# A one-layer language-model tower on one core: block 0's layer norms split between two engines, the first recurring pass written out

## Chip, core and metric

The kernel runs on one core of a Trainium2 chip. The metric is the device time of one launch in microseconds (us), as the median of several runs. The core's engines are TensorE (PE in the profile), VectorE (DVE), ScalarE (ACT), GpSimd (POOL) and SyncE (SP), which here only issues DMAs. Each engine works through its own list of instructions in order, and waits on semaphores for the others.

## What is computed

The input is an (8, 1024) array of token numbers: L = 8 positions, N = 1024 sequences, width 256. The reference, cut to what matters:

```
h = take(table, x)                                   # (8, 1024, 256)
h = h + attention(layernorm(h))                      # 16 heads of 16, softmax over the 8 positions
h = h + ffn(layernorm(h))

attention:  qkv = x @ Wqkv.T + b;  softmax(q k / 4) v @ Wo.T + bo
ffn:        scores = sigmoid(x @ Wg.T); 2 of 4 groups, then 4 of 16 experts by scores + bias
            weights = 2.5 * scores / sum(scores of the 4)
            sum over experts of weight * W2[e] relu(W1[e] x)^2  +  Ws2 relu(Ws1 x)^2
layernorm:  (x - mean) / sqrt(var + 1e-5)
```

Everything is float32. Each operand of most matmuls is split into a high part (rounded to fp32r) and a low part (the rest), and three products are summed.

## The kernel before

**Tiling.** The 1024 sequences are cut into B = 16 blocks of 64, so that a block has 512 tokens, held either as rows (128 partitions x 4 rows j x 256) or transposed (128 partitions x 2 halves kh x 512). For each block: `gather` (GpSimd, L395) fetches the rows into `xin`; `norm_stats` (VectorE, L755) takes the statistics; `rstd_of` (GpSimd, L405) makes scale and shift from them in eight small operations, a power and a product; `normalise` (ScalarE, L538) writes the four normalised rows; `transpose_rows` (TensorE, L1177) transposes them into PSUM; `transposed_hi` (ScalarE, L549) and `transposed_lo` (VectorE, L763) split them; `qkv` (L1191) and `qkv_out` (L558) give q, k and v. `product` (VectorE, L288) multiplies q and k into a ring of four buffers, `score` (L1206) sums over a head, `scores_max`, `exponent`, `scores_sum`, `probs_high`, `probs_low` are the softmax. `spread_probs` (L1222) spreads probabilities over lanes, `weighted_values` (L769) multiplies them with v, `sum_of` (L304, on GpSimd or VectorE) sums over positions, `attention_hi`/`_lo` split the result, `out_projection` (L1240) and `residual` (L897) give h1, with the statistics of the second norm right behind. The second norm takes the same path (w = 1) to xT2. Then `logits`, `logits_back`, 22 steps of `route` on VectorE, `weights_transpose` and `weights_out`, a store and reloads of the expert weights by SP (L355, L349), and for each of 18 hidden tiles (2 shared, 16 experts) `up` (L1145), `weigh` on VectorE (L731), `square` on ScalarE (L524), `hidden_lo` on VectorE (L742) and `down` (L1160).

**Weights.** They come in 14 pieces. SP issues their loads (L324 to L345), from piece 4 on after the first block's rows have landed. `weight_hi(k)` (ScalarE, L519) rounds a piece and `weight_lo(k)` (VectorE, L726) makes the rest. The pieces are staged in buffers that are used for other things later: the ring holds pieces 4 to 8, so the first product waits until nine pieces are done (RING_FREE, L281), and SP stores block 0's expert weights only after thirteen (L379).

**Order of the work.** Each engine has a list written out by hand, which has two parts: a start-up list for block 0, block 1 and the beginning of the expert work of block 0, and then `for b in range(B + 1): period(b)`. One `period(b)` interleaves the expert work of block b with the second half of the attention of block b + 1 and the first half of that of block b + 2. The start-up lists stand at L489 (GpSimd), L673 (ScalarE), L1056 (VectorE) and L1386 (TensorE). `warm(4)` (L1277) in TensorE's list is four matmuls on a weight piece whose result is never read; there are 17 such calls.

**GpSimd's start.** It issues the gathers of blocks 0 and 1 (eight in all, L495 and L497), then does `rstd_of(0, 0)`, `constants_small` (masks), `constants_spread` (a memset and four selects on a 128 x 1024 buffer, L457) and `bias_in(0)` (L427), which adds the output bias to `xin` and waits for the broadcasts of the biases.

Of the kernel before, what the change touches and what calls it, by code (L numbers as in the profile page):

```python
# [5 lines left out]
def lm_tower_layer(nc: bass.Bass, ids, table, wqkv_t, bqkv, wo_t, bo, wg_t, bias_corr,  # L6
# [8 lines left out]
    f32 = mybir.dt.float32  # L15
# [44 lines left out]
    with ctx:  # L60
# [99 lines left out]
        xn_ready = [sem("xn1_ready"), sem("xn2_ready")]  # L160
        xT_mm = [sem("xT1_mm"), sem("xT2_mm")]
# [224 lines left out]
        def _(pool):  # L386
# [18 lines left out]
            def rstd_of(w, blk):  # L405
                st, m = stats[w], mv[w]
                tt, ts = nc.gpsimd.tensor_tensor, nc.gpsimd.tensor_scalar
                pool.wait_ge(ln_stats[w], nth(blk, 1, 1))
# [3 lines left out]
                pool.wait_ge(ln_step[w], nth(blk, 5, 1))  # L412
# [3 lines left out]
                pool.wait_ge(ln_step[w], nth(blk, 5, 2))  # L416
                tt(m[:, 1, :], m[:, 1, :], m[:, 1, :], ALU.mult).then_inc(ln_step[w], 1)
                pool.wait_ge(ln_step[w], nth(blk, 5, 3))
                tt(m[:, 2, :], m[:, 2, :], m[:, 1, :], ALU.add).then_inc(ln_step[w], 1)
                pool.wait_ge(ln_step[w], nth(blk, 5, 4))  # L420
                if blk >= 1:
                    pool.wait_ge(xn_ready[w], nth(blk, 1, 0))
                tt(rstd[w][:, :], m[:, 2, :], half_neg[:, :], ALU.pow).then_inc(ln_step[w], 1)
                pool.wait_ge(ln_step[w], nth(blk, 5, 5))
                tt(nmr[w][:, :], m[:, 3, :], rstd[w][:, :], ALU.mult).then_inc(ln_rstd[w], 1)

            def bias_in(blk):  # L427
# [3 lines left out]
                pool.wait_ge(xn_ready[0], nth(blk, 1, 1))  # L431
                par = blk % 2
# [76 lines left out]
            bias_in(1)  # L509
# [3 lines left out]
            for b in range(B + 1):  # L513
                period(b)
# [3 lines left out]
        def _(act):  # L518
# [19 lines left out]
            def normalise(w, blk):  # L538
# [5 lines left out]
                for j in range(TT):  # L544
# [4 lines left out]
            def transposed_hi(w, blk):  # L549
                act.wait_ge(xT_mm[w], nth(blk, 1, 1))  # L550
# [5 lines left out]
                nc.scalar.copy(dst[:, :, :], src[:, :, :]).then_inc(xT_hi[w], 1)  # L556
# [133 lines left out]
            weight_hi(9)  # L690
            qkv_out(0, 5)
            spread_in()
# [5 lines left out]
            weight_hi(11)  # L698
            transposed_hi(0, 1)
            attention_hi(0, 1)  # L700
            qkv_out(1, 0)
            qkv_out(1, 1)
            qkv_out(1, 2)
            qkv_out(1, 3)
            weight_hi(12)
            qkv_out(1, 4)
            normalise(1, 0)
            weight_hi(13)
            transposed_hi(1, 0)
            logits_out(0)  # L710
            router(0)
# [771 lines left out]
```

## Time and profile before

| | us |
|---|---|
| median of 3 runs | 1248.94 |
| lowest, highest | 1248.72, 1251.21 |
| profiled execution, its time | 1247.4 |
| profiled execution, span of the core's instructions | 1245.7 |
| busy in that span: TensorE, VectorE, ScalarE, GpSimd | 1198.8, 1021.5, 597.0, 503.8 |

The profile is of one execution. All times in its rows are counted from the first instruction. A timeline row merges like instructions that follow one another on an engine (x4) and gives start, duration, engine, line, operation, what is written from what, and in brackets how long the engine had been idle before and what released it. `<-` in a name reads "from". The granted clock (PEclk) is TensorE's, as a share of full speed.

### The profile page before, as it was taken

What the parts mean: (1) busy time and instruction counts of PE and PEld (TensorE: products, weight loads), DVE (VectorE), ACT (ScalarE), POOL (GpSimd) and SP (SyncE); (2) the same over time, 40 slices, a digit from 0 to 9 for tenths busy, and PEclk for the clock granted to TensorE, in tenths of its full rate; (3) what the DMA queues carried; (4) which work ended last, traced back from release to release, by engine and by line L of the source; (5) the groups of instructions that cost most, each with busy time, mean ns of one, the idle gap of its engine ahead of it and who ended that gap; (6) DMA issues with size and microseconds to landing.
All of it is one profiled execution on the core that took longest, in us unless ns stands there. A gap on an engine that the chain in (4) does not pass through costs nothing.

```text
span 1245.7 us, 19787 instructions
## 1 busy us (share of the span) xinstructions
PE 1198.8 (96%) x7428; PEld 1013.5 (81%) x7428; DVE 1021.5 (82%) x1732; ACT 597.0 (48%) x1056; POOL 503.8 (40%) x717
## 2 busy tenths in 40 slices
PE   3689999999999999999999999999999999999998
PEld 3357888797888878788887888879788887878897
DVE  4989798897979889787888978788897878888643
ACT  4334645454464545446454544544455454444443
POOL 7355435163542516354251635425263451516000
PEclk9898999999999999999999999999999999999999
DMA  6002222032222213222121322213132221312232
GB/s 225 1 18 69 70 68 89 31 105 67 86 69 69 75 45 104 68 87 68 57 82 51 103 68 86 69 30 108 52 102 69 72 82 34 104 35 91 64 108 63
DMA packets 34127, 91.64 MB, mean 74 GB/s; under 512 B 4720, under 2 KB 13296, under 8 KB 34032
## 3 DMA queue, kind: packets, MB, share of 16 engines
q1 hardware_dynamic: 30960, 81.99, 20.2%
q0 software_dynamic: 3072, 8.39, 2.2%
q8 instruction: 58, 0.95, 0.3%
q14 instruction: 37, 0.30, 0.1%
HBM read 81.46 MB, written 8.91 MB: 73 GB/s over the span
## 4 chain that ended last, share of the span: by engine, by line
PE 93%; DVE 4%; POOL 1%; issue 1%; ACT 1%; DMA 0%; DVEq 0%; POOLq 0%; ACTq 0%; SPq 0%
PE psY L1170 33%; PE psH L1155 32%; PE psB L1201 10%; PE psB L1217 4%; PE psA L1248 4%; PE psB L1236 2%; PE psA L1236 2%; PE psA L1260 1%; DVE ring L288 1%; PE psB L1187 1%; PE psA L1187 1%; PE psY L1281 1%; POOL xin L401 1%; PE psA L1274 1%; PE psA L1267 0%
## 5 line engine op out<-in xcount | busy, mean ns | idle before, releaser
L1170 PE MATMUL psY<-w_hi,hid_hi 128*128 128x256 f32 x1152 | 326.1, 283 | 0.0
L1170 PE MATMUL psY<-w_hi,hid_lo 128*128 128x256 f32 x1152 | 323.8, 281 | 0.0
L1170 PE MATMUL psY<-w_lo,hid_hi 128*128 128x256 f32 x1152 | 323.3, 281 | 0.0
L534 ACT ACTIVATE p_sb<-r_sb 128x512 f32<-128x512 f32 x288 | 181.2, 629 | 255.1 <-DVE r_sb L739 212.5
L536 ACT ACTIVATE hid_hi<-r_sb 128x512 fp32r<-128x512 f32 x288 | 180.0, 625 | 215.4 <-PE psY L1170 212.8
L739 DVE SCALAR_TENSOR_TENSOR r_sb<-psH,cwB 128x512 f32<-128x512 f32 x256 | 173.7, 684 | 83.3 <-PE psH L1155 79.1
L1170 PEld LDWEIGHTS psY<-w_hi,hid_hi 128*128 128x128 f32 x1152 | 217.0, 188 | 20.9 <-DVE hid_lo L745 11.7
L1155 PE MATMUL psH<-xT_hi,w_hi 128*128 128x512 f32 x576 | 230.8, 401 | 1.2 <-ACT r_sb L529 1.2
L1155 PE MATMUL psH<-xT_hi,w_lo 128*128 128x512 f32 x576 | 228.5, 397 | 0.0
L1155 PE MATMUL psH<-xT_lo,w_hi 128*128 128x512 f32 x576 | 227.8, 395 | 0.0
L1170 PEld LDWEIGHTS psY<-w_lo,hid_hi 128*128 128x128 f32 x1152 | 216.9, 188 | 9.3
L745 DVE TENSOR_TENSOR hid_lo<-p_sb,hid_hi 128x512 fp32r<-128x512 f32 x288 | 199.0, 700 | 22.9 <-ACT hid_hi L536 20.9
L1170 PEld LDWEIGHTS psY<-w_hi,hid_lo 128*128 128x128 f32 x1152 | 216.8, 188 | 0.0
L310 POOL TENSOR_TENSOR ring<-ring 128x512 f32<-128x512 f32 x94 | 144.1, 1533 | 93.0 <-DVE ring L777 92.1
L438 POOL TENSOR_TENSOR w_rec<-w_sum,half_neg 128x4 f32<-128x4 f32 x16 | 24.2, 1514 | 380.3 <-DVE w_sum L846 380.3
L288 DVE TENSOR_TENSOR ring<-q_sb,k_sb 128x1024 f32<-128x1024 f32 x128 | 153.4, 1224 | 4.1 <-ACT k_sb L567 3.9
L1155 PEld LDWEIGHTS psH<-xT_hi,w_hi 128*128 128x128 f32 x576 | 108.8, 189 | 33.5 <-DVE r_sb L739 10.9
L1155 PEld LDWEIGHTS psH<-xT_hi,w_lo 128*128 128x128 f32 x576 | 108.8, 189 | 25.6
L1155 PEld LDWEIGHTS psH<-xT_lo,w_hi 128*128 128x128 f32 x576 | 109.0, 189 | 19.1
L777 DVE TENSOR_TENSOR ring<-psA,v_sb 128x1024 f32<-128x1024 f32 x64 | 78.1, 1220 | 10.0 <-PE psA L1236 9.9
L777 DVE TENSOR_TENSOR ring<-psB,v_sb 128x1024 f32<-128x1024 f32 x64 | 77.9, 1218 | 7.2 <-PE psB L1236 7.2
L401 POOL DMA_INDIRECT xin<-table,idx x64 | 73.3, 1145 | 19.1 <-issue 17.2
(138 smaller groups left out, 1854.3 us busy)
## 6 DMA issues: line engine op xcount, KB each, us to landing
cwB<-cw_dram SPq DMA_DIRECT2D x128, 512.0 KB, 3.7
out<-h SPq DMA_DIRECT2D x32, 256.0 KB, 3.2
xin<-table,idx POOLq DMA_INDIRECT x64
ring<-w_t SPq DMA_DIRECT2D x4, 256.0 KB, 6.3
h<-w_t SPq DMA_DIRECT2D x2, 512.0 KB, 7.6
ring<-w_t SPq DMA_DIRECT2D x1, 512.0 KB, 6.6
p_sb<-w_t SPq DMA_DIRECT2D x2, 256.0 KB, 7.0
cwB<-w_t SPq DMA_DIRECT2D x1, 512.0 KB, 7.8
```

Source lines behind the costliest of these rows:

```text
L288: ns.tensor_tensor(ring[:, t % 4, :, :].rearrange("p l (m n) -> p l m n", m=L), qv.unsqueeze(2).to_broadcast([P, 2, L, NN]), kv.unsqueeze( ...
L310: ns.tensor_tensor(a[:, :, 0:4, :], a[:, :, 0:4, :], a[:, :, 4:8, :], ALU.add).then_inc(sum_step[who], 1)
L401: nc.gpsimd.indirect_dma_start(xin[b % 2][:, j, :], None, table, bass.IndirectOffsetOnAxis(idx[:, b * TT + j:b * TT + j + 1], 0)).then_inc ...
L534: nc.scalar.activation(p_sb[:, n % 2, :], r_sb[:, n % 2, :], ACT.Square)
L536: nc.scalar.activation(hid[0][:, n % R, :], r_sb[:, n % 2, :], ACT.Square).then_inc(hid_hi, 1)
L739: nc.vector.scalar_tensor_tensor(r_sb[:, n % 2, :], psH[:, n % 2, :], 0.0, cwB[:, (r // QN) % 2, r % QN, :], ALU.max, ALU.mult).then_inc(w ...
L745: nc.vector.tensor_tensor(hid[1][:, n % R, :], p_sb[:, n % 2, :], hid[0][:, n % R, :].bitcast(f32), ALU.subtract).then_inc(hid_lo, 1)
L777: nc.vector.tensor_tensor(ring[:, t % 4, :, :], ps[:, :, :], v_sb[:, ih, :].unsqueeze(1).to_broadcast([P, 2, T]), ALU.mult).then_inc(av_re ...
L1155: last = nc.tensor.matmul(psH[:, n % 2, :], W1[a][:, kh, e, :], x[c][:, kh, :], start=(kh == 0 and (a, c) == PASSES[0]), stop=(kh == KH - ...
L1170: last = nc.tensor.matmul(psY[:, j // 2, (j % 2) * D:(j % 2 + 1) * D], hid[a][:, e % R, j * P:(j + 1) * P], W2[b][:, e, :], start=(e == 0 ...
L1201: last = nc.tensor.matmul(psB[:, n % 2, :], WQKV[a][:, kh, 2 * c + ih, :], xT1[b][:, kh, :], start=(kh == 0 and (a, b) == PASSES[0]), stop ...
L1217: last = nc.tensor.matmul(psB[row:row + 32, 0, :], head_sum[:, lp, :], ring[:, (KH * lp + ih) % 4, li, :], start=(lp == 0), stop=(lp == LP ...
```

## The change

**Normalisation of block 0, both layer norms.** `norm_stats` calls the new `first_norm` for block 0. The mean and variance come from `bn_aggr` on VectorE, GpSimd only raises to the power -1/2, VectorE makes the shift, and then VectorE normalises rows 2 and 3 while ScalarE normalises rows 0 and 1. TensorE signals after the first four of eight transposes, ScalarE makes the high part in two halves and VectorE the low part in two halves. Later blocks go the old way.

**Order.** On GpSimd `constants_small` and `rstd_of(0, 0)` come ahead of the gathers of block 1, and `bias_in(0)` ahead of `constants_spread`. On the other engines several steps of the start-up lists change places, and the first recurring pass, `period(0)`, becomes part of the list, with an order of its own; the loop starts at 1. TensorE's list has 17 calls of `warm(4)` before and after, at other places: one instead of two after the first transposes, three ahead of the transposes of the second norm of block 0, none behind the first `spread_probs(1, ...)`.

The diff, with the lists cut to the places that the prediction speaks of:

```
             def rstd_of(w, blk):
+                if blk == 0:
+                    pool.wait_ge(first_step[w], 2)
+                    tt(rstd[w][:, :], m[:, 2, :], half_neg[:, :], ALU.pow).then_inc(first_root[w], 1)
+                    return
...
 # GpSimd's list
             gather_first(0)
+            constants_small()
+            rstd_of(0, 0)
             gather_first(1)
-            rstd_of(0, 0)
-            constants_small()
+            bias_in(0)
             constants_spread()
-            bias_in(0)
             sum_of(0, 0)
...
             gather(2)
-            bias_in(1)
             root_of_sum(0)
             sum_of(1, 0)
             sum_of(1, 1)
-            for b in range(B + 1):
+            sum_of(1, 2)
+            bias_in(1)
+            rstd_of(0, 2)
...
+            for b in range(1, B + 1):
                 period(b)
...
             def normalise(w, blk):
-                for j in range(TT):
+                for j in range(TT if blk > 0 else TT // 2):
...
             def transposed_hi(w, blk):
+                if blk == 0:
+                    to, ps = (xT1[0], psB) if w == 0 else (xT2[0][0], psA)
+                    act.wait_ge(half_mm[w], 1)
+                    nc.scalar.copy(to[:, 0, :], ps[:, 0, :]).then_inc(half_hi[w], 1)
                 act.wait_ge(xT_mm[w], nth(blk, 1, 1))
...
-                nc.scalar.copy(dst[:, :, :], src[:, :, :]).then_inc(xT_hi[w], 1)
+                if blk == 0:
+                    nc.scalar.copy(dst[:, 1, :], src[:, 1, :]).then_inc(xT_hi[w], 1)
+                else:
+                    nc.scalar.copy(dst[:, :, :], src[:, :, :]).then_inc(xT_hi[w], 1)
...
 # ScalarE's list
+            weight_hi(4)
             normalise(0, 0)
-            weight_hi(4)
             weight_hi(5)
+            transposed_hi(0, 0)
             weight_hi(6)
-            transposed_hi(0, 0)
             weight_hi(7)
             qkv_out(0, 0)
             weight_hi(8)
...
+            weight_hi(11)
             probs_high(0)
             normalise(0, 1)
+            transposed_hi(0, 1)
             attention_hi(0, 0)
...
             def norm_stats(w, blk):
+                if blk == 0:
+                    first_norm(w)
+
+            def first_norm(w):
+                src, dst = (xin[0], k_sb) if w == 0 else (h1[0], o_sb)
+                m = mv[w]
...
+                dve.wait_ge(ln_stats[w], 1)
+                for j in range(TT):
+                    last = nc.vector.bn_aggr(pairs[:, j, :], stats[w][:, j, :])
+                last.then_inc(first_step[w], 1)
+                dve.wait_ge(first_step[w], 1)
+                nc.vector.tensor_scalar(m[:, 2, :], var, EPS, None, ALU.add).then_inc(first_step[w], 1)
+                dve.wait_ge(first_root[w], 1)
+                nc.vector.scalar_tensor_tensor(nmr[w][:, :], mean, -1.0, rstd[w][:, :], ALU.mult, ALU.mult
+                                               ).then_inc(ln_rstd[w], 1)
+                dve.wait_ge(ln_rstd[w], 1)
...
+                for j in range(TT // 2, TT):
+                    last = nc.vector.tensor_scalar(d[:, j, :], src[:, j, :], rstd[w][:, j:j + 1], nmr[w][:, j:j + 1],
+                                                   ALU.mult, ALU.add)
+                last.then_inc(first_rows[w], 1)
...
             def transposed_lo(w, blk):
+                if blk == 0:
+                    dve.wait_ge(half_hi[w], 1)
+                    nc.vector.tensor_tensor(dst[1][:, 0, :], src[:, 0, :], dst[0][:, 0, :].bitcast(f32), ALU.subtract)
+                    dve.wait_ge(xT_hi[w], 1)
+                    nc.vector.tensor_tensor(dst[1][:, 1, :], src[:, 1, :], dst[0][:, 1, :].bitcast(f32),
+                                            ALU.subtract).then_inc(xT_lo[w], 1)
...
 # VectorE's list
+            weight_lo(10)
+            probs_low(0)
             norm_stats(0, 1)
-            probs_low(0)
...
+            transposed_lo(0, 1)
             weighted_values(0, 7)
-            transposed_lo(0, 1)
...
             product(1, 2)
+            transposed_lo(1, 0)
             product(1, 3)
...
-            hidden_lo(0, 0)
+            weight_lo(12)
             weighted_values(1, 0)
+            hidden_lo(0, 1)
             weighted_values(1, 1)
-            for b in range(B + 1):
+            weighted_values(1, 2)
+            weighted_values(1, 3)
+            norm_stats(0, 2)
+            weigh(0, 2)
...
+            attention_lo(1, 1)
+            product(2, 0)
+            hidden_lo(0, 7)
+            weight_lo(13)
+            residual(1)
+            weigh(0, 8)
...
             def transpose_rows(w, blk):
+                if blk == 0:
+                    pe.wait_ge(first_rows[w], 1)
...
+                    if blk == 0 and kh == 0:
+                        last.then_inc(half_mm[w], 1)
...
 # TensorE's list
             transpose_rows(0, 0)
             warm(4)
-            warm(4)
             qkv(0, 0)
...
             qkv(0, 4)
+            qkv(0, 5)
             score(0, 0)
...
+            qkv(1, 2)
             out_projection(0)
...
+            down(0, 0)
             spread_probs(1, 0)
             weights_transpose(0)
             spread_probs(1, 1)
-            warm(4)
-            for b in range(B + 1):
+            spread_probs(1, 2)
+            spread_probs(1, 3)
+            down(0, 1)
+            spread_probs(1, 4)
+            spread_probs(1, 5)
+            up(0, 3)
+            up(0, 4)
...
+            qkv(2, 4)
+            up(0, 10)
...
+            for b in range(1, B + 1):
                 period(b)
```

## Rows read from the trace of the kernel before

**Rows 1.** The chain that ended last, by engine.
```profile
PE 93%; DVE 4%; POOL 1%; issue 1%; ACT 1%; DMA 0%; DVEq 0%; POOLq 0%; ACTq 0%; SPq 0%
```

**Rows 2.** Windows by stage; the first line names the columns.
```profile
core 0: us, PE busy (x) PEld busy (x) DVE busy (x) ACT busy (x) POOL busy (x), PEclk, DMA share, GB/s
...
67.17:104.44 37.27, 31.60 (x147) 21.79 (x147) 31.16 (x59) 15.46 (x27) 14.78 (x16) 0.86 0.05 15
...
104.90:175.80 70.90, 70.23 (x436) 58.92 (x435) 60.89 (x107) 34.20 (x62) 31.34 (x44) 1.00 0.21 68
175.80:249.00 73.20, 73.20 (x462) 62.22 (x461) 62.35 (x107) 36.42 (x66) 31.08 (x44) 1.00 0.23 73
```

**Rows 3.** Waits of TensorE from 105 us on, longest of three (total, times, longest).
```profile
PE psA L1187 <- ACT o_sb L545: 1.3, 1, 1.3
```

**Rows 4.** Timeline of the head: start us, duration us, engine, line, operation, idle before.
```profile
10.55 1.41 DVE L760 BATCH_NORM_STATS2 stats<-xin 128x6 f32<-128x256 f32 x4 [1.92 <-DMA xin<-table,idx]
...
12.81 0.95 POOL L401 DMA_INDIRECT xin<-table,idx  x1 [0.30 <-issue]
...
15.74 1.05 POOL L423 TENSOR_TENSOR rstd<-mv,half_neg 128x4 f32<-128x4 f32 x1
...
19.33 1.94 PE L1187 MATMUL psB<-ident,k_sb 128*128 128x128 f32 x8 [19.33 <-POOL not_first L453]
20.93 3.34 PE L1281 MATMUL psY<-wqkv_hi 128*128 128x512 f32 x8
```

**Rows 5.** Timeline, VectorE beside GpSimd; a line's durations (ns min/median/max); VectorE's products.
```profile
21.20 1.57 DVE L729 TENSOR_TENSOR w_lo<-ring,w_hi 128x1024 fp32r<-128x1024 f32 x1 [0.18 <-ACT w_hi L522]
22.70 1.21 DVE L766 TENSOR_TENSOR xT_lo<-psB,xT_hi 128x1024 fp32r<-128x1024 f32 x1
...
27.44 2.35 DVE L729 TENSOR_TENSOR w_lo<-ring,w_hi 128x1024 fp32r<-128x1024 f32 x1 [1.94 <-ACT w_hi L522]
29.90 9.17 DVE L288 TENSOR_TENSOR ring<-q_sb,k_sb 128x1024 f32<-128x1024 f32 x8
...
26.30 2.41 POOL L433 TENSOR_TENSOR xin<-xin,bo_sb 128x1024 f32<-128x1024 f32 x1
...
L463 POOL TENSOR_SCALAR_AFFINE_SELECT r_sb<-r_sb x4: 845/1488/1602, 20.4 to 24.6; 128x512 f32<-128x512 f32 x4
```

**Rows 6.** Issues on SP's queue; page part 6: issues, size, median us to landing.
```profile
13.76 0.65 SPq L343 DMA_DIRECT2D bias_corr_sb<-bias_corr  x1
14.45 1.32 SPq L330 DMA_DIRECT2D ring<-w_t  x2
...
ring<-w_t SPq DMA_DIRECT2D x4, 256.0 KB, 6.3
...
bias_corr_sb<-bias_corr SPq DMA_DIRECT2D x1, 8.0 KB, 6.7
```

**Rows 7.** Timeline of VectorE and ScalarE, block 0's second half and block 1's products.
```profile
65.91 1.21 DVE L766 TENSOR_TENSOR xT_lo<-psB,xT_hi 128x1024 fp32r<-128x1024 f32 x1
...
76.07 1.41 DVE L760 BATCH_NORM_STATS2 stats<-h 128x6 f32<-128x256 f32 x4
...
86.80 1.22 DVE L766 TENSOR_TENSOR xT_lo<-psA,xT_hi 128x1024 fp32r<-128x1024 f32 x1
...
91.46 1.13 DVE L796 TENSOR_TENSOR lgt<-lg 128x64 f32<-128x64 f32 x1 [1.17 <-ACT lg L601]
...
98.07 0.41 DVE L824 MAX8 top<-cho 128x8 f32<-128x16 f32 x4
...
81.36 2.08 ACT L545 ACTIVATE o_sb<-h,nmr,rstd 128x256 f32<-128x256 f32 x4
```

**Rows 8.** Timeline from the end of block 1's probabilities.
```profile
103.00 1.39 DVE L884 TENSOR_TENSOR probs<-s_sb,probs 64x512 fp32r<-64x512 f32 x2
...
112.14 0.69 DVE L739 SCALAR_TENSOR_TENSOR r_sb<-psH,cwB 128x512 f32<-128x512 f32 x1 [0.85 <-DMA cwB<-cw_dram]
...
113.59 0.40 PE L1155 MATMUL psH<-xT_hi,w_hi 128*128 128x512 f32 x1
```

More of the change, by code:

```diff
@@ L1103, in _ @@
             product(1, 5)
-            weight_lo(12)
-            transposed_lo(1, 0)
+            route(0, 0)
             product(1, 6)
-            weight_lo(13)
-            route(0, 0)
+            route(0, 1)
             product(1, 7)
-            route(0, 1)
             route(0, 2)
@@ L1121, in _ @@
             route(0, 11)
+            scores_max(1)
             route(0, 12)
             route(0, 13)
+            route(0, 14)
             scores_sum(1)
-            route(0, 14)
             route(0, 15)
+            hidden_lo(0, 0)
             route(0, 16)
@@ L1133, in _ @@
             route(0, 21)
-            hidden_lo(0, 0)
+            weight_lo(12)
             weighted_values(1, 0)
+            hidden_lo(0, 1)
             weighted_values(1, 1)
-            for b in range(B + 1):
+            weighted_values(1, 2)
+            weighted_values(1, 3)
+            norm_stats(0, 2)
+            weigh(0, 2)
+            weigh(0, 3)
+            weighted_values(1, 4)
+            weigh(0, 4)
+            weigh(0, 5)
+            weighted_values(1, 5)
+            hidden_lo(0, 2)
@@ new lines, in _ @@
+            sum_of(1, 3)
+            hidden_lo(0, 3)
+            hidden_lo(0, 4)
+            attention_lo(1, 0)
+            weigh(0, 6)
+            weighted_values(1, 6)
+            hidden_lo(0, 5)
+            weigh(0, 7)
+            weighted_values(1, 7)
+            transposed_lo(0, 2)
+            sum_of(1, 7)
+            hidden_lo(0, 6)
+            attention_lo(1, 1)
[4 more added lines that the diff above has]
+            weigh(0, 8)
@@ new lines, in _ @@
+            weigh(0, 9)
+            hidden_lo(0, 8)
+            product(2, 1)
+            product(2, 2)
+            product(2, 3)
+            product(2, 4)
+            weigh(0, 10)
+            hidden_lo(0, 9)
+            transposed_lo(1, 1)
+            weigh(0, 11)
+            weigh(0, 12)
+            hidden_lo(0, 10)
+            product(2, 5)
+            route(1, 0)
+            hidden_lo(0, 11)
+            route(1, 1)
+            product(2, 6)
+            route(1, 2)
+            weigh(0, 13)
@@ new lines, in _ @@
+            product(2, 7)
+            route(1, 3)
+            route(1, 4)
+            hidden_lo(0, 12)
+            route(1, 5)
+            route(1, 6)
+            scores_max(2)
+            hidden_lo(0, 13)
+            route(1, 7)
+            weigh(0, 14)
+            route(1, 8)
+            route(1, 9)
+            route(1, 10)
+            weigh(0, 15)
+            route(1, 11)
+            hidden_lo(0, 14)
+            route(1, 12)
+            weigh(0, 16)
+            route(1, 13)
@@ new lines, in _ @@
+            route(1, 14)
+            scores_sum(2)
+            hidden_lo(0, 15)
+            route(1, 15)
+            route(1, 16)
+            route(1, 17)
+            route(1, 18)
+            weigh(0, 17)
+            hidden_lo(0, 16)
+            route(1, 19)
+            probs_low(2)
+            route(1, 20)
+            route(1, 21)
+            hidden_lo(0, 17)
+            weighted_values(2, 0)
+            hidden_lo(1, 0)
+            weighted_values(2, 1)
+            for b in range(1, B + 1):
@@ L1393, in _ @@
             qkv(0, 4)
+            qkv(0, 5)
             score(0, 0)
-            qkv(0, 5)
+            warm(4)
             score(0, 1)
@@ L1409, in _ @@
             warm(4)
+            warm(4)
             spread_probs(0, 6)
```

169 lines of the change are left out of this document (135 added, 34 removed).

## The prediction

> **What bounds the kernel now.** I read the chain that ended last first, since it says which engine sets the end: TensorE has 93% of it [rows 1]. Next the windows, by stage. From the second pass on TensorE is busy 73.20 us of 73.20, and in the first pass (104.90 to 175.80) 70.23 of 70.90, while VectorE has ten free microseconds or more; in the stretch before, 67.17 to 104.44, it is busy 31.60 of 37.27 us at a granted clock of 0.86, with VectorE at 31.16 [rows 2]. The waits of TensorE after 105 us then have three entries, the longest 1.3 us [rows 3]. So the kernel has two parts: up to about 104 us VectorE and chains of short steps bound it, with TensorE often idle or on `warm` matmuls that compute nothing; behind that TensorE's fixed work runs without a gap. A microsecond taken out before 104 us is a microsecond off the end, unless TensorE gets a gap later. I forecast by following the first 113 us. The profiled execution has a span of 1245.7 us and a time of 1247.4 us, 1.5 us under the median of 1248.94; the sum is made on the first and shifted by 1.5.
>
> **Head: first normalisation (0 to 39 us).** Today the statistics end at 11.96 us (10.55 + 1.41), but GpSimd still issues the second block's gathers until 13.76, then needs eight small operations up to 15.74 (about 0.25 each), the power of 1.05 and a product, to 17.1; behind ScalarE's four rows (2.08 in the second norm [rows 7]) the transposes start at 19.33 [rows 4]. The change puts those gathers behind the power. On VectorE four `bn_aggr` come in, which no row shows: nearest are the four MAX8 of 0.41 in all [rows 7], the other end the four statistics themselves, 1.41; I take 0.41, because the inputs are 6 elements wide. With one `tensor_scalar` (0.2), the power (1.05), one product (0.2) and five hand-overs of some 0.07, scale and shift stand at 14.2 instead of 17.1. ScalarE does two rows (half of 2.08) and VectorE two beside it (at most 0.35 each by the statistics' rate): transposes at 15.4, 3.9 earlier. The halves let the high part follow the first four transposes, so xT_lo is there at 18.3; four warm matmuls (today eight take 3.34 [rows 4], so 1.7) end at 18.7: the first qkv moves from 24.3 to 18.7.
>
> That is not what the head gains. The products also need the ring's weight piece 8. Its loads are issued from 14.45 on and take 6.3 us in the middle [rows 6], so it lands near 21.6; cast (1.04) and qkv_out(0,1) (0.7) follow, at 23.4. On VectorE pieces 6, 7 and 8 queue. `bias_in(0)` now starts when its broadcasts land, issued 13.76, 0.65 long, 6.7 to landing: 20.5 [rows 6]. Today piece 8 takes 2.35 beside it [rows 5]; tomorrow piece 7 meets it. `constants_spread` moves behind it, to about 23 to 30. Product 0 so starts between 24.9 (ScalarE and the load) and 26.0 (with the blocks beside `bias_in`); I take 25.4 against 29.90.
>
> The eight products take 9.17 [rows 5] in free air; three of the four selects now lie beside them. A piece beside a select took 1.57, while an instruction of the same size with a PSUM operand took 1.21 [rows 5]: 0.35 extra. A select took 0.845 at least and 1.6 at most. I take 0.6 a select, 1.9 with the memset's end: last product 36.5 instead of 39.07, **-2.6 us**. Bounds: -5.0 with no collision, -0.5 if each of four products takes the 2.35 of the piece beside `bias_in`.
>
> The Trainium skill ("SBUF — State Buffer", section "Who interferes with whom") says that a VectorE instruction with two SBUF inputs and a GpSimd instruction that reads SBUF exclude each other for a whole instruction, and speaks against this move. By it three selects cost 2.5 us instead of 1.9; the trace agrees: `bias_in` ended at 28.71 and piece 8, begun at 27.44, ended 1.1 later [rows 5].
>
> **Middle (39 to 75 us).** Moving `norm_stats(0,1)` (1.4) behind `probs_low(0)` fills the 1.3 us in which VectorE waits for the first spread, and weight_lo(10) takes its old place beside probs_high: nothing gained or lost here, 1.1 saved later. transposed_lo(0,1), at 65.91 today [rows 7], passes one weighted_values (1.2), so qkv(1,0) starts 1.1 earlier. Out-projection now stands behind three qkv but these start earlier; the residual stays behind weight_lo(11): **-1.0**, bounds 0 and -1.2.
>
> **Second normalisation (76 to 104 us).** Today statistics end 77.48, GpSimd's chain gives the shift at 81.3, ScalarE starts at 81.36 and VectorE's low part at 86.80, behind product 5 and weight_lo(12) [rows 7]. After: chain of 2.1 instead of 3.8, rows 1.04 instead of 2.08, transposes 3.7 earlier (the twelve warm matmuls ahead end 0.3 before); VectorE, held 2.1 us for the power, does products 1 and 2 and then the two low halves of about 0.65: logits 5.2 earlier (82.9 without the head's gain). From there to the end of probs_low(1) VectorE needs 16.4 us today (88.02 to 104.39 [rows 7, 8]). After: three products more (+3.45), weight_lo(13) gone (-1.15), the 1.17 us wait for the logits filled, the first route step 0.9 shorter without `bias_in(1)` beside it [rows 7], hidden_lo(0,0) in front (+0.6): 17.6. So probs_low(1) ends at 100.5, 3.9 earlier with the middle, of which **-2.9** here. Bounds: -1.5 (if `bn_aggr` costs 1.41 and TensorE's steps run at half speed) and -4.
>
> **Recurring pass 0 (104 to 176 us).** Its clock starts at T = end of probs_low(1). Today up(0,4) starts at T + 9.2, right after weigh(0,2), which waits for the expert weights' table until T + 7.75 [rows 8]; TensorE has done five spreads, up 3, down 0 and 1, and four warm matmuls. After: weight_lo(12) (1.2) stands before the first weighted value, four of these and the statistics before weigh(0,2), which ends at T + 8.8; TensorE has done the same and one spread more (0.47): **-0.8**. Bounds +3 and -2. weight_lo(13) goes into VectorE's free time. The table's DMAs keep their place, after cwT, since weight_lo(12) ends before cwT is ready. The semaphores themselves I cost at nothing.
>
> Sum: -2.6 - 1.0 - 2.9 - 0.8 = -7.3; 1247.4 - 7.3 = 1240.1, and 1241.6 as a median.
>
> **Rivals.**
> A. The forecast, 1238 to 1244: 0.68.
> B. The head gives nothing: weight_hi(4) now stands before the normalisation on ScalarE, and its load is issued at 10.54; a landing after 14.2, or the collisions at their upper bound, eats it. Speaking for it: loads issued two microseconds later take 6.3 [rows 6]; against: the DMA engines carry far less at that moment, and the loads at piece 8 hide 2 us of it anyway. -7.3 + 2.6 = -4.7: 1244.2. The skill's rule above, taken in full, ends here too. 0.11.
> C. TensorE at the lower of its two levels. It ran matmuls at 0.42 instead of 0.23 us in the warm group at 20.93 [rows 4], and had 0.86 granted in 67 to 104 [rows 2]. It idles some 2 us in the first 9 of the new pass; if the low level reaches eight microseconds into the pass, 4 are lost: 1245.6. 0.09.
> D. No change: the gain is handed back by gaps in the pass that was written out, 1248.9. Against it: ten free microseconds of VectorE [rows 2]. 0.06.
> E. Slower. Place: up(0,10), which needs weigh(0,8), now behind residual(1), product(2,0) and weight_lo(13) on VectorE. By my count weigh(0,8) ends at T + 35 and TensorE gets there at T + 37.3, 2.3 of slack. Each microsecond beyond costs one; it decides for slower from 2.3 + 7.3 + 2.5 = 12 us of delay, i.e. if all VectorE work of that stretch took a third longer. With 14 us: 1251.0 or more. 0.06.
>
> **How the numbers follow.** A measurement can tell 0.2% (2.5 us) from no change. A, B and C are faster, 0.88; D same, 0.06; E slower, 0.06. The range of 1238 to 1246.5 holds A to C but for their tails, and leaves out D and E.
>
> **What would show it.** Right: POOL's power at 12.8 instead of 15.74; transposes near 15.4; first product near 25.4 and the last one's end near 36.5; products of 1.5 to 2.1 us beside the selects; first logits near 80; probs_low(1) ending near 98; up(0,4) some 9 us later; in the pass TensorE idle for at most 2 us. Wrong: a long wait of ScalarE before its first row (B), a granted clock under 1.00 after the start of the pass (C), waits of TensorE on r_sb or hid_lo in the 70 us after it (D, E).

## The result, and the profile after

The changed kernel takes 1240.35 us, the median of 4 runs (1238.81 to 1241.86), against 1249.30 for the kernel before (1248.72 to 1251.21): a ratio of 0.9927, with a 95% interval of 0.9913 to 0.9941. The forecast was 1241.6 us in a range of 1238.0 to 1246.5.

The profiled execution of the changed kernel has a time of 1241.86 us and a span of 1240.1; that of before 1247.4 and 1245.7. The two profiles so differ by 5.5 us and the medians by 9.0: the profile of before is one of its faster executions, that of after the slowest of its four. The second profile of the changed kernel, below, shows what part of this the trace can explain. All steps below are read from the profiles.

| mark in the trace, us | before | after | after, a second profile |
|---|---|---|---|
| transposes of the first norm start | 19.33 | 15.22 | 15.18 |
| first product starts | 29.90 | 24.57 | 24.54 |
| first maximum of the softmax (`scores_max(0)`) | 40.37 | 38.16 | 37.26 |
| residual(0) | 74.82 | 71.30 | 70.42 |
| probs_low(1) ends (T) | 104.39 | 96.93 | 96.06 |
| `weights_transpose(1)`, the end of the first recurring pass | 175.9 | 170.4 | 169.0 |
| end of the span | 1245.7 | 1240.1 | 1238.7 |

From the second pass on each pass takes 73.1 to 73.2 us in all three (the last one 62.3 to 62.4), so whatever stands at 170 us stands at the end. By stage, against before: head -2.2, middle -1.3, second normalisation -3.9, first recurring pass **+1.9** us, sum -5.5.

The page of after: the chain that ended last, by engine, and the busy line. They answer to [rows 1]; VectorE's share of the chain went from 4 to 6%, TensorE's busy time is the same to a tenth.

```profile
PE 1198.8 (97%) x7428; PEld 1012.1 (82%) x7428; DVE 1028.3 (83%) x1750; ACT 593.5 (48%) x1054; POOL 505.2 (41%) x699
...
PE 91%; DVE 6%; issue 1%; POOL 1%; ACT 1%; DMA 0%; POOLq 0%; DVEq 0%; SPq 0%
```

VectorE's timeline in the head of after (start, duration, operation, idle before and its releaser):

```profile
12.02 0.38 DVE L838 BATCH_NORM_AGGREGATE mv<-stats 128x2 f32<-128x6 f32 x4
...
14.03 0.73 DVE L848 TENSOR_SCALAR k_sb<-xin,rstd,nmr 128x256 f32<-128x256 f32 x2
...
18.76 5.70 DVE L794 TENSOR_TENSOR w_lo<-ring,w_hi 128x1024 fp32r<-128x1024 f32 x3 [0.25 <-ACT w_hi L545]
24.57 11.42 DVE L293 TENSOR_TENSOR ring<-q_sb,k_sb 128x1024 f32<-128x1024 f32 x8
...
38.16 0.69 DVE L959 TENSOR_REDUCE s_max<-psB 128x64 f32<-128x512 f32 x1 [1.03 <-PE psB L1400]
```

GpSimd's in the same stretch:

```profile
12.75 1.04 POOL L415 TENSOR_TENSOR rstd<-mv,half_neg 128x4 f32<-128x4 f32 x1 [1.75 <-DVE mv L841]
...
18.88 3.37 POOL L445 TENSOR_TENSOR xin<-xin,bo_sb 128x1024 f32<-128x1024 f32 x1
...
23.29 7.12 POOL L475 TENSOR_SCALAR_AFFINE_SELECT r_sb<-r_sb 128x512 f32<-128x512 f32 x4
```

The four aggregates take 0.38 us (taken: 0.41) and the power starts at 12.75 (forecast 12.8). The three pieces take 5.70 instead of 3 x 1.2 because `bias_in(0)` meets them, and is itself stretched to 3.37 from 2.41 [rows 5] (2.92 in the second profile, where it started 0.4 later). The eight products take 11.42 instead of 9.17 [rows 5], 2.25 more, beside the four selects. The last one ends at 35.99; the forecast was 36.5.

TensorE in after, the last three scores of the head; then windows of after and of before around them (busy us and count of TensorE, its weight loads, VectorE, ScalarE, GpSimd, then the granted clock, the DMA share and GB/s):

```profile
31.60 1.07 PE L1400 MATMUL psB<-ring,head_sum 128*32 128x512 f32 x8 [1.34 <-DVE ring L293]
33.87 1.93 PE L1400 MATMUL psB<-ring,head_sum 128*32 128x512 f32 x8 [1.20 <-DVE ring L293]
36.14 1.93 PE L1400 MATMUL psB<-ring,head_sum 128*32 128x512 f32 x8 [0.34 <-DVE ring L293]
```

```profile
30.00:39.00 9.00, 5.19 (x26) 0.64 (x24) 7.94 (x8) 2.57 (x3) 0.41 (x1) 0.69 0.01 2
```

```profile
33.00:42.00 9.00, 6.29 (x38) 2.26 (x34) 8.59 (x9) 2.75 (x4) 0.00 (x0) 1.00 0.01 2
```

The eight matmuls of each of the last two scores take 1.93 us instead of 1.07: TensorE had been waiting for stretched products, and its clock fell to the lower of its two levels, 1.2 GHz (0.69 on the mean of these nine microseconds, 1.00 before). The last score thus ends 0.9 later. In the second profile of the same kernel the scores took 1.06 us behind the same waits (1.20 and 1.21), and the softmax began 0.9 earlier; the marks of the table ahead of it differ by at most 0.04.

The second norm in after, VectorE. It answers to [rows 7]:

```profile
71.30 1.23 DVE L1000 TENSOR_TENSOR h<-psA,xin 128x1024 f32<-128x1024 f32 x1 [1.07 <-issue]
72.56 1.41 DVE L825 BATCH_NORM_STATS2 stats<-h 128x6 f32<-128x256 f32 x4
...
78.83 0.68 DVE L856 TENSOR_TENSOR xT_lo<-psA,xT_hi 128x512 fp32r<-128x512 f32 x1
...
95.54 1.39 DVE L980 TENSOR_TENSOR probs<-s_sb,probs 64x512 fp32r<-64x512 f32 x2
```

From the residual to the low part it is 7.5 us instead of 12.0, and to the end of probs_low(1) 25.6 instead of 29.6.

Windows of after: the 32.5 us ahead of the pass, the pass, the next one, and two stretches of the pass's opening. They answer to [rows 2].

```profile
65.00:97.50 32.50, 29.57 (x161) 20.58 (x159) 29.19 (x68) 14.40 (x26) 12.67 (x6) 1.00 0.06 17
97.50:170.40 72.90, 70.52 (x419) 58.15 (x419) 63.58 (x107) 34.49 (x62) 33.89 (x45) 0.98 0.20 66
170.40:243.60 73.20, 73.20 (x462) 62.27 (x461) 63.70 (x108) 36.36 (x67) 32.09 (x44) 1.00 0.23 73
...
103.00:104.00 1.00, 1.00 (x7) 1.00 (x6) 1.00 (x2) 0.00 (x0) 1.00 (x1) 0.50 0.87 315
104.00:105.00 1.00, 1.00 (x6) 1.00 (x6) 1.00 (x4) 0.00 (x0) 0.84 (x3) 0.50 0.77 315
```

TensorE's waits in the pass (longest of those from 96 us on):

```profile
PE psA L1419 <- DVE ring L873: 1.0, 1, 1.0
...
PE psA L1419 <- ACT cwT L603: 0.7, 1, 0.7
PE psB L1419 <- DVE probs L980: 0.6, 1, 0.6
```

The pass that was written out is 72.9 us instead of 70.9: TensorE idles 2.4 of them (0.7 before [rows 2]), at its start, between spreads, and for three microseconds around 103 us it has 0.50 granted.

### The profile page after: what moved, and what is told of

It is laid out like the page before. It is cut to its first block, busy times and chain, and to the rows that moved or that the text cites. A ratio compares the mean times of both kernels' runs of the same rounds, so it can differ in the third digit from the quotient of the medians.

```text
span 1240.1 us, 19788 instructions
## 1 busy us (share of the span) xinstructions
PE 1198.8 (97%) x7428; PEld 1012.1 (82%) x7428; DVE 1028.3 (83%) x1750; ACT 593.5 (48%) x1054; POOL 505.2 (41%) x699
## 4 chain that ended last, share of the span: by engine, by line
PE 91%; DVE 6%; issue 1%; POOL 1%; ACT 1%; DMA 0%; POOLq 0%; DVEq 0%; SPq 0%
PE psY L1349 33%; PE psH L1334 32%; PE psB L1384 10%; PE psB L1400 4%; PE psA L1431 4%; PE psA L1419 2%; PE psB L1419 2%; DVE ring L293 1%; PE psA L1443 1%; PE psB L1368 1%; PE psA L1368 1%; DVE ring L873 1%; DVE w_lo L794 1%; PE psA L1457 1%; PE psA L1450 0%
## 5 line engine op out<-in xcount | busy, mean ns | idle before, releaser
L810 DVE TENSOR_TENSOR hid_lo<-p_sb,hid_hi 128x512 fp32r<-128x512 f32 x288 | 201.7, 709 | 23.9 <-ACT hid_hi L559 22.1
L1334 PEld LDWEIGHTS psH<-xT_hi,w_lo 128*128 128x128 f32 x576 | 108.3, 188 | 25.4
L406 POOL DMA_INDIRECT xin<-table,idx x64 | 77.5, 1212 | 18.9 <-issue 16.8
```

What stands on the lines that cost most here:

```text
L406: nc.gpsimd.indirect_dma_start(xin[b % 2][:, j, :], None, table, bass.IndirectOffsetOnAxis(idx[:, b * TT + j:b * TT + j + 1], 0)).then_inc ...
L810: nc.vector.tensor_tensor(hid[1][:, n % R, :], p_sb[:, n % 2, :], hid[0][:, n % R, :].bitcast(f32), ALU.subtract).then_inc(hid_lo, 1)
L1334: last = nc.tensor.matmul(psH[:, n % 2, :], W1[a][:, kh, e, :], x[c][:, kh, :], start=(kh == 0 and (a, c) == PASSES[0]), stop=(kh == KH - ...
```

## The experiments

The kernel before ran again beside each group; its medians were 1248.82, 1248.18, 1247.69 and 1248.79 us. "T" is the end of probs_low(1) in the experiment's own profile (before 104.39, after 96.93). Line numbers are each kernel's own.

### Group 1: which part earns the gain

**The new normalisation alone**: the functions of after, the four lists of before.

```
-            constants_small()
-            rstd_of(0, 0)
             gather_first(1)
-            bias_in(0)
+            rstd_of(0, 0)
+            constants_small()
             constants_spread()
+            bias_in(0)
...
-            for b in range(1, B + 1):
+            for b in range(B + 1):
                 period(b)
```

> The new code for block 0 (bn_aggr, shared rows, halves) with all four lists of the kernel before. Theory 1 (the gain is the earlier end of probs_low(1), and each part gives what lies on the path): GpSimd's gathers of block 1 still stand ahead of the power, so the transposes start near 16.2 instead of 19.33 and the first product near 27 instead of 29.9; in the second norm VectorE's low part stands behind product 5 and weight_lo(12) as before, so the faster chain gives nothing there. Total about -3 us, ratio 0.9975. Theory 2 (the normalisation is the whole gain): -7 us or more, ratio 0.994 or below. Rival: nothing, because VectorE is held for the power: ratio 1.000.

1246.92 us, ratio 0.9991 (0.9978 to 1.0005). The first norm's transposes start at 16.24 (3.1 earlier, still behind the second block's gathers), but the softmax only 1.1 earlier, at 39.24, and T is 100.95. In the second norm the low part starts at 84.21, 2.6 earlier, no more than the residual's own 2.7: it stays behind product 5 and weight_lo(12), so the norm gains nothing up to there.

**The order alone**: all four lists of after, the functions of before.

> The old normalisation code with all four new lists (so the written-out pass too). Theory 1: the chain of the first norm starts at 12 instead of 13.8 and one warm group is gone, the selects still meet the products; low part of the second norm before product 3; about -4 to -5 us, ratio 0.996 to 0.997, and together with the norm-only kernel about the whole change. Theory 2 (normalisation is the whole gain): ratio 0.999 to 1.001.

1248.92 us, ratio 1.0003 (0.9991 to 1.0014). VectorE's timeline says why:

```profile
76.67 2.34 DVE L288 TENSOR_TENSOR ring<-q_sb,k_sb 128x1024 f32<-128x1024 f32 x2
87.16 1.22 DVE L812 TENSOR_TENSOR xT_lo<-psA,xT_hi 128x1024 fp32r<-128x1024 f32 x1 [8.15 <-ACT xT_hi L567]
88.30 3.48 DVE L288 TENSOR_TENSOR ring<-q_sb,k_sb 128x1024 f32<-128x1024 f32 x3
```

The new order puts transposed_lo(1, 0) behind two products, which fits a normalisation that is ready by then. The old one isn't: VectorE stands 8.15 us with five products queued behind. By the medians either part alone gives 1.9 us, with an interval that holds 1.000, or nothing; the two together give 9. (Between its profile and that of before, the normalisation alone gives 3.4 us, at T and at the end of the span.) Order and code are one change.

**The loop's first pass**: after, with `period(0)` of the loop instead of the pass written out (weight_hi(13), weight_lo(13) and bias_in(1) ahead of it, down(0, 0) inside it).

```
             sum_of(1, 1)
-            sum_of(1, 2)
             bias_in(1)
...
-            for b in range(1, B + 1):
+            for b in range(B + 1):
                 period(b)
...
             weighted_values(1, 1)
-            weighted_values(1, 2)
-            weighted_values(1, 3)
-            norm_stats(0, 2)
-            weigh(0, 2)
...
             weight_lo(13)
...
```

> The changed kernel, but with the first recurring pass taken from the loop as before (start-up list cut before down(0,0), weight pieces 12 and 13 and bias_in(1) ahead of the loop). The forecast's step (the written-out pass gives 0.8 us) wants it about 1 us slower than the changed kernel, ratio to before 0.9935. The reading of the trace of after (the pass took 72.9 us between two weights_transpose although 2.35 us of matmuls were taken out of it, so its opening loses some 2.8 us) wants it equal or up to 2 us faster, ratio 0.991 to 0.993, with TensorE idle under 1 us in the first 10 us behind the end of probs_low(1).

1242.87 us, ratio 0.9958 (0.9944 to 0.9972); T is 97.05, and the pass takes 74.4 us against 72.9. TensorE's two longest waits from 96 us on:

```profile
PE psB L1290 <- DVE probs L934: 2.8, 1, 2.8
PE psA L1302 <- DVE xT_lo L944: 2.3, 1, 2.3
```

The first ends at T, in front of the pass: TensorE has no down(0, 0) there to fill it, and VectorE sets T, so it costs nothing. The second lies in the pass (for the transposed attention of block 1), and the pass written out hasn't got it. That pass is worth 1.5 us in this pair of profiles and 0.3% in the ratios. But the loop's pass takes 70.9 us in the kernel before and in the first experiment, at 1.00 granted; here the clock is at the lower level from about 99.3 to 102.7 us, and TensorE is busy 71.35 us in the pass for 70.24 there. How much is owed to the list, how much to piece 13, which now stands in VectorE's opening, and how much to the clock, this run doesn't separate.

### Group 2: where the pass loses, and the first repair of the order

**The changed kernel once more**, unchanged.

> The changed kernel itself, to stand beside the next three on the same chip. Ratio 0.991 to 0.994 as in its first measurement.

1239.13 us, ratio 0.9927 (0.9913 to 0.9941). Its second profile stands in the table above; its pass takes 72.3 us.

**Something for TensorE to do in the opening**:

```
             spread_probs(1, 1)
+            up(0, 3)
             spread_probs(1, 2)
-            spread_probs(1, 3)
             down(0, 1)
+            spread_probs(1, 3)
             spread_probs(1, 4)
             spread_probs(1, 5)
-            up(0, 3)
```

> The changed kernel with up(0,3) and down(0,1) moved ahead in the opening of the written-out pass: up(0,3) behind spread_probs(1,1), down(0,1) behind spread_probs(1,2). Theory: the opening of the pass loses some 2.8 us because TensorE idles between spreads (2.4 us) and then runs down(0,1) at the lower level; filled, up(0,4) starts near T + 9 instead of T + 10.4 (T is the end of probs_low(1)) and the pass between two weights_transpose takes 71.0 to 71.8 us instead of 72.9: 1 to 2 us faster than the changed kernel, ratio 0.990 to 0.992. Rival: VectorE's list decides, the idle time only moves: pass of 72.5 to 73, ratio as the changed kernel.

1240.57 us, ratio 0.9941 (0.9927 to 0.9955), not told apart from the changed kernel. The pass is 71.5 us with 1.00 granted throughout, shorter than the 72.9 and 72.3 of the two profiles of the changed kernel but longer than the 70.6 that the unchanged list takes at 1.00 (next experiment). TensorE idled 2.8 us in it all the same, of which 1.3 now in front of the expert matmuls:

```profile
PE psH L1334 <- DVE r_sb L804: 1.3, 1, 1.3
PE psA L1419 <- DVE ring L873: 0.8, 1, 0.8
```

VectorE's weigh(0, 2) paces TensorE here. The gap that was filled early came back later: against the unchanged list at the same clock the edit costs 0.9 us.

**The selects beside the first norm instead of the products**:

```
             rstd_of(0, 0)
+            constants_spread()
             gather_first(1)
             bias_in(0)
-            constants_spread()
```

> The changed kernel with constants_spread ahead of the gathers of block 1 on GpSimd, so that the four selects lie beside nothing that VectorE reads twice, and bias_in meets the first products. Theory (collisions cost what they took in the trace: 11.42 instead of 9.17 us for eight products, 0.9 more for pieces 7 and 8): the selects' 2.2 us go and bias_in's block of one product by at most 2.4 comes: last product's end 34.5 to 35.5 instead of 36.0, ratio 0.9 us better than the changed kernel or the same. Rival: later gathers make block 1's rows late; nothing is seen of that before norm_stats(0,1) at 45.

1240.44 us, ratio 0.9938 (0.9922 to 0.9953). The collisions moved, they didn't go away. VectorE:

```profile
13.96 1.83 DVE L848 TENSOR_SCALAR k_sb<-xin,rstd,nmr 128x256 f32<-128x256 f32 x2
...
26.05 10.53 DVE L293 TENSOR_TENSOR ring<-q_sb,k_sb 128x1024 f32<-128x1024 f32 x7 [0.62 <-ACT k_sb L597]
```

Two rows of the norm take 1.83 instead of 0.73, and `bias_in(0)`, now at 26.26, stretches seven products to 10.53. The norm's rows were stretched although they read only one large input from SBUF, which this experiment's expectation had not reckoned with. The softmax starts at 38.74, behind a last score at the lower level (1.94 us), and T is 96.04. The pass took 70.6 us, with 1.00 granted throughout.

**Order alone, with the low part behind product 5 again**:

```
             product(1, 2)
-            transposed_lo(1, 0)
             product(1, 3)
             product(1, 4)
             product(1, 5)
+            transposed_lo(1, 0)
```

> The order-only kernel (old normalisation code, new lists) with transposed_lo(1,0) moved behind product(1,5) on VectorE, about where it stood before. Theory: order-only gained nothing because VectorE waited 8.15 us at that place for the slow second normalisation, with products 3 to 7 behind it; moved back, the maximum of block 1 comes near 95.5 instead of 99.0 and probs_low(1) ends near 103.5 instead of 106.7: ratio 0.997 to 0.998 instead of 1.000. Rival (nothing to do with that place): ratio 1.000.

1254.11 us, ratio 1.0049 (1.0035 to 1.0063): slower, not mended. Products 4 and 5 wait 8.75 us for a ring buffer, which score(1, 0) has to free, since TensorE has the second norm's transposes in front of score(1, 0). VectorE, then TensorE's wait:

```profile
88.45 2.36 DVE L288 TENSOR_TENSOR ring<-q_sb,k_sb 128x1024 f32<-128x1024 f32 x2 [8.75 <-PE psB L1346]
```

```profile
PE psA L1316 <- ACT o_sb L556: 5.5, 1, 5.5
```

### Group 3: the meetings of VectorE and GpSimd, the halves, and a second repair

**No meeting**: selects held back until the last product, `bias_in(0)` until probs_low(0).

```
             gather_first(1)
-            bias_in(0)
+            pool.wait_ge(prod_ready[1], 4)
             constants_spread()
+            pool.wait_ge(probs_lo, 1)
+            bias_in(0)
...
             weight_hi(9)
-            spread_in()
             qkv_out(0, 5)
             weight_hi(10)
             exponent(0)
+            spread_in()
```

> The changed kernel with constants_spread held until the last product of block 0 is done and bias_in(0) until probs_low(0) is done, so that neither meets a VectorE instruction with two SBUF inputs; ScalarE copies the spread mask behind exponent(0). Theory (meetings cost the first eight products 2.2 us and weight pieces 7 and 8 about a microsecond): pieces 6 to 8 at 1.22 each, first product 23.5 to 24, eight products in 9.2, last one's end near 33 instead of 36.0, probs_low(1) 2 to 3 us earlier than 96.1 to 96.9: ratio 0.990 to 0.991. Rival (something else is late next, the scores or the mask): ratio as the changed kernel, 0.9927.

1238.64 us, ratio 0.9925 (0.9913 to 0.9937). VectorE:

```profile
18.79 2.36 DVE L796 TENSOR_TENSOR w_lo<-ring,w_hi 128x1024 fp32r<-128x1024 f32 x2 [0.25 <-issue]
...
26.00 8.04 DVE L293 TENSOR_TENSOR ring<-q_sb,k_sb 128x1024 f32<-128x1024 f32 x7 [0.62 <-ACT k_sb L599]
...
42.22 1.39 DVE L982 TENSOR_TENSOR probs<-s_sb,probs 64x512 fp32r<-64x512 f32 x2 [1.30 <-ACT probs L616]
```

Every instruction is back at its free duration and the softmax starts at 35.33, 2.8 earlier than in after (1.9 earlier than in its second profile). VectorE then waits 1.30 for ScalarE, which has spread_in and weight_hi(11) ahead of probs_high(0). T is 95.20, and the pass, at 1.00 granted, 70.6 us. The profile so gains 2.6 to 4.0 us in span on the two of the changed kernel (1236.1 against 1238.7 and 1240.1), but the ratio is not told apart from its 0.9927. The windows of the pass in this kernel:

```profile
95.80:166.40 70.60, 68.72 (x419) 56.62 (x419) 62.49 (x107) 34.60 (x62) 34.24 (x45) 1.00 0.21 68
```

It holds as many matmuls as after's (419) and takes 68.72 us of TensorE for them instead of 70.52, with 1.9 idle instead of 2.4. That prices the lower level in after's pass: 1.8 us more of busy time for the same work, and 0.5 more of idle, with no edit to the pass. The other profiles bear it out. Ten of them have this list for the pass: seven with 1.00 granted throughout take 70.5 to 70.7 us, with TensorE busy 68.6 to 68.8, and three whose clock fell in the opening (the changed kernel twice, and the order with its second repair, below) take 72.3 to 72.9, busy 70.2 to 70.5.

**Order alone, with TensorE's scores in front too** (to the last kernel of group 2):

```
-            transpose_rows(1, 0)
             score(1, 0)
-            logits(0)
+            transpose_rows(1, 0)
             score(1, 1)
+            logits(0)
```

> The order-only kernel with both places put back that bet on a fast second normalisation: TensorE does score(1,0) ahead of transpose_rows(1,0) and score(1,1) ahead of logits(0), VectorE does transposed_lo(1,0) behind product(1,5). Theory: with the old normalisation it is these two waits that eat the gain of the order; maximum of block 1 near 95.5, end of probs_low(1) near 103.5 (order-only 106.7, TensorE's place left as it was 110.1), ratio 0.996 to 0.998. Rival: the new order gives nothing before the pass in any case: ratio 1.000 or above.

1251.89 us, ratio 1.0028 (1.0016 to 1.0040). The wait moved to ScalarE's list, where `normalise(1, 0)` stands ahead of the qkv_out(1, 4) that score(1, 0) needs:

```profile
82.02 2.07 ACT L556 ACTIVATE o_sb<-h,nmr,rstd 128x256 f32<-128x256 f32 x4 [6.79 <-POOL nmr L425]
84.00 0.67 ACT L578 ACTIVATE v_sb<-psB,bqkv_sb 128x512 f32<-128x512 f32 x1
```

**The changed kernel without halves**: the whole high and low part of block 0 in one instruction each.

```
-                if blk == 0:
-                    to, ps = (xT1[0], psB) if w == 0 else (xT2[0][0], psA)
-                    act.wait_ge(half_mm[w], 1)
-                    nc.scalar.copy(to[:, 0, :], ps[:, 0, :]).then_inc(half_hi[w], 1)
                 act.wait_ge(xT_mm[w], nth(blk, 1, 1))
...
-                    nc.scalar.copy(dst[:, 1, :], src[:, 1, :]).then_inc(xT_hi[w], 1)
```

> The changed kernel without the halves: one high copy and one low part for block 0 in both norms, the rest of the change kept. Theory: the first qkv starts some 0.6 us later (19.3) but the first product hardly (0 to 0.3), since the load of piece 8 sets it; in the second norm logits start 0.6 us later and products 3 to 7 with them: 0.6 us in all, ratio 0.9927 to 0.9937, not told apart from the changed kernel by the times but by the marks of the trace. Rival: the halves carry the change: 2 us or more, ratio 0.9945.

1240.80 us, ratio 0.9944 (0.9931 to 0.9957): 0.17% above the changed kernel's ratio, with intervals that overlap. In the trace the first qkv starts at 19.64 instead of 18.66 and the first product at 25.90 instead of 24.57, but the products then meet fewer selects and the last one ends only 0.9 later, at 36.87. The softmax starts at 38.17, as in after, but the scores ran at full clock here:

```profile
37.02 1.06 PE L1386 MATMUL psB<-ring,head_sum 128*32 128x512 f32 x8 [1.20 <-DVE ring L293]
```

The profile to compare with is so the second one of the changed kernel, whose scores took 1.06 too: against it the softmax is 0.9 later and T, 97.32, is 1.3 later. The halves are worth some 1.3 us at T, and in the comparison with after the clock hides it.

### Group 4: a third repair, and the best version

**Order alone, with ScalarE's list mended as well** (to the second repair):

```
-            normalise(1, 0)
             qkv_out(1, 4)
+            normalise(1, 0)
```

> The order-only kernel with three places put back: the two of the last experiment and, on ScalarE, qkv_out(1,4) ahead of normalise(1,0). In the trace of the last one ScalarE waited 6.8 us for the shift in front of normalise(1,0), qkv_out(1,4) came at 84.0 behind it, and score(1,0) needs it. Theory (all three lists bet on a fast second normalisation, ScalarE's place is the one that holds the scores): score(1,0) near 78 to 80, products 4 and 5 no longer wait 7 us, maximum of block 1 near 95, probs_low(1) ending at 102.5 to 104 (order-only 106.7), ratio 0.996 to 0.998. Rival: 1.000 or above again, then a fourth place or the order as such.

1250.96 us, ratio 1.0018 (1.0007 to 1.0029). The scores are early now and no product waits, yet the low part comes at 89.28. GpSimd's chain, which makes scale and shift, and VectorE beside it:

```profile
76.24 1.11 POOL L409 TENSOR_TENSOR mv<-stats 128x4 f32<-128x4 f32 x1 [10.93 <-DVE stats L806]
77.32 1.20 POOL L410 TENSOR_SCALAR mv<-stats 128x4 f32<-128x4 f32 x1
78.48 1.16 POOL L411 TENSOR_SCALAR mv<-stats 128x4 f32<-128x4 f32 x1
79.72 0.20 POOL L413 TENSOR_TENSOR mv<-mv 128x4 f32<-128x4 f32 x1
...
81.35 1.06 POOL L417 TENSOR_TENSOR mv<-mv 128x4 f32<-128x4 f32 x1
```

```profile
76.08 3.48 DVE L288 TENSOR_TENSOR ring<-q_sb,k_sb 128x1024 f32<-128x1024 f32 x3
79.99 2.36 DVE L288 TENSOR_TENSOR ring<-q_sb,k_sb 128x1024 f32<-128x1024 f32 x2 [0.43 <-PE psB L1346]
89.28 1.22 DVE L812 TENSOR_TENSOR xT_lo<-psA,xT_hi 128x1024 fp32r<-128x1024 f32 x1 [6.93 <-ACT xT_hi L567]
```

A GpSimd operation on four elements a partition takes 0.2 us while VectorE pauses (79.56 to 79.99) and 1.1 to 1.2 when products run beside it: one per product. In the kernel before, VectorE was waiting for k_sb while this chain ran, and all eight took about 0.2. VectorE of the kernel before, right behind its statistics, and two of the chain's operations:

```profile
79.98 5.77 DVE L288 TENSOR_TENSOR ring<-q_sb,k_sb 128x1024 f32<-128x1024 f32 x5 [2.50 <-ACT k_sb L567]
```

```profile
77.56 0.21 POOL L409 TENSOR_TENSOR mv<-stats 128x4 f32<-128x4 f32 x1 [12.31 <-DVE stats L760]
...
79.19 0.20 POOL L419 TENSOR_TENSOR mv<-mv 128x4 f32<-128x4 f32 x1
```

The new order takes that pause away; the new code, with only the power left on GpSimd and VectorE itself held for it, doesn't need it.

**No meeting, and ScalarE free for the probabilities** (to the no-meeting kernel):

```
             spread_in()
-            weight_hi(11)
             probs_high(0)
+            weight_hi(11)
```

> The no-meeting kernel with weight_hi(11) behind probs_high(0) again: there ScalarE did the spread mask and piece 11 in a row and VectorE waited 1.3 us for probs_high(0). Theory: weighted_values(0,0) at 43.7 instead of 44.96, probs_low(1) ends 93.9 to 94.5 (95.2), 2 to 3 us ahead of the changed kernel; if the clock stays up in the opening of the pass the span is 1234.5 to 1236; ratio 0.990 to 0.992. Rival: as the changed kernel, 0.9927.

1237.35 us (1236.75 to 1240.48), ratio 0.9914 (0.9901 to 0.9927): the lowest median of all, about 2 us under the changed kernel's of 1239.13, but the intervals of the two ratios overlap, so that the times don't tell them apart; the trace does. VectorE's wait for probs_high(0) is 0.35 instead of 1.30, T is 94.02 (96.93 and 96.06 in the changed kernel), and the pass takes 70.7 us. Of the kernels here it is the one to keep.

## Why the prediction held, and where it did not

- **Bound**: as said. From the second pass on TensorE sets the time, and the marks at 170 us decide.
- **Head, -2.6 forecast, -2.2 measured** (-3.1 in the second profile). The chain of the norm came out to within 0.2 us at every mark (power 12.75, transposes 15.22, first qkv 18.66). The first product came at 24.57 for 25.4 (24.9 to 26.0): piece 8 had landed by 21.47, and VectorE's pieces beside `bias_in(0)` set it. The selects cost 2.25 for the 1.9 taken. `bias_in(0)` started at 18.88 for 20.5. What the sum lacked is the 0.9 us of scores at 1.2 GHz: rival C's mechanism, in a place where it wasn't priced.
- **The rule of the Trainium skill** ("SBUF — State Buffer", section "Who interferes with whom"), by which VectorE with two SBUF inputs and GpSimd reading SBUF exclude each other for whole instructions, would by the prediction's estimate have made that 2.5, for three selects. Four met pieces and products, so that the rule at 0.845 each would make it 3.4 (an estimate); the products lost 2.25, 0.56 a select. So the sizes here lie under the rule taken in full. That the two exclude each other the other runs bear out: without meetings every duration is back, and in group 4 a tiny GpSimd operation lasts as long as the product beside it.
- **Middle, -1.0 forecast, -1.3 measured**, 0.1 past the bound.
- **Second normalisation, -2.9 forecast, -3.9 measured**, at the bound of -4. The logits came 5.7 us earlier than the head's gain alone explains (5.2 forecast; both include the middle's), and the term "17.6" from the low part's end to T was mis-sized: it took 16.8 (80.11 to 96.93), and its own parts add up to 17.2 and not 17.6. T was 96.93 for "near 98".
- **The failed step is "Recurring pass 0: -0.8": it measured +1.9 in one profile of the changed kernel and +1.4 in the other**, inside the bounds and of the other sign. weigh(0, 2) ended where the count had it, at T + 8.9 for T + 8.8 (105.14 + 0.67), but up(0, 4) started at T + 10.4. I counted TensorE's steps at full rate between waits, and its idle time in the pass at no more than 2 us (2.4). The 12 matmuls of down(0, 1) came every 0.213 us, at 1.2 GHz; in the kernel without meetings, at 1.00 granted, every 0.118. Where the clock stayed up, the same list took 70.6 us, 0.3 less than before: the list by itself gave the sign of the forecast, and what it took for nothing is the lower level, 1.7 to 2.3 us.
- **Rival C** so came true in part, at about 2.3 us instead of 4, on top of the forecast and not instead of it. B was wrong in its place (ScalarE had cast piece 4 by 13.79 and then waited 0.24 for the shift) and its collisions cost 2.25, well under its bound. D and E did not come: TensorE has no wait on r_sb or hid_lo over 0.5 us after T. E's price was off: with 14 us of delay its own terms give 1253.3, not 1251.0.
- **The total**, 1240.35 for 1241.6, is nearer than its terms, by luck: against a difference of 5.5 us between the profiles 7.3 was forecast, and the medians differ by 9.0. One kernel's executions spread over 7 us (before: 1244.2 to 1251.2), and the two profiled ones stood on opposite sides of their medians. The pass's miss of 2.7 was made up for by the gains of the second norm and the middle beyond their terms (1.3) and by this spread.
- **Not settled**: whether the new order can gain anything without the new normalisation. Three repairs, at VectorE's, TensorE's and ScalarE's lists, each found the next wait; the last one is GpSimd's chain, which wasn't tried apart.

## What to carry to other kernels

When an order is rewritten around a step made faster, price the two as one: here each alone gave 1.9 us (not told apart from nothing) or nothing, together 9. Before moving a GpSimd chain beside VectorE's two-input work, count one VectorE instruction for each tiny GpSimd one, and look first for work that can wait (here masks and a bias not needed for 20 us). And where TensorE idles between short steps, forecast the stretch at both of its clock levels: the same list took 70.5 to 70.7 or 72.3 to 72.9 us. Compare marks of two kernels only where the clock was the same.

## What the runs showed of the hardware

- With the same instructions and the same gaps, TensorE's clock fell in some executions and not in others: 0.50 granted for three to four microseconds in the opening of the pass in both profiles of the changed kernel, 1.00 in seven kernels with the same list for the pass (selects early, without halves, the two without meetings, and the order alone, as it is and with its first and third repair). What decides between them these traces don't tell.
- The eight small GpSimd operations of a norm take 1.8 us in the kernel before (77.56 to 79.39) or, beside products, 6.4 (76.24 to 82.68 in group 4).
- Four selects of 128x512 take 3.82 us with VectorE's two-input work out of the way (last kernel) and 7.12 beside it:

```profile
34.97 3.82 POOL L475 TENSOR_SCALAR_AFFINE_SELECT r_sb<-r_sb 128x512 f32<-128x512 f32 x4
42.58 2.37 POOL L445 TENSOR_TENSOR xin<-xin,bo_sb 128x1024 f32<-128x1024 f32 x1 [3.78 <-DVE probs L982]
```
